# Attention block of one core: P@V for two key tiles in every second step, and products regrouped by odd and even steps

## The reference

```
xn  = layernorm(x)
qkv = xn @ qkv_w + qkv_b                    # 16 heads of 16 channels
a   = softmax(q k^T * 16**-0.5)             # 512 x 512 for each head and row
y1  = (a v) @ proj_w + proj_b
g, u = xn @ w_gate.T / 127, xn @ w_up.T / 127   # integer weights, 768 hidden
y2  = (silu(g) * u) @ w_down.T / 127
out = x + y1 + y2
```

## Time and profile before

| | |
|---|---|
| time before, median of 3 runs | 574.96 us (574.86 to 575.86) |
| the profiled execution | 576.71 us, its span 574.9 us |
| TensorE busy | 97% of the span |
| VectorE, ScalarE, GpSimd busy | 81%, 73%, 53% |
| granted TensorE clock | 0.994 |

### The profile page before, as it was taken

One profiled execution on the slowest core, in us unless ns is written; L12 is line 12 of the kernel. 1 busy time (PEld: TensorE's weight loads), 2 busy tenths in 40 slices (PEclk: granted clock), 3 DMA queues, 4 the chain that ended last, 5 costly groups with the idle time before them and its releaser, 6 DMA issues.

```text
span 574.9 us, 13815 instructions
## 1 busy us (share of the span) xinstructions
PE 555.6 (97%) x4844; PEld 334.2 (58%) x4844; DVE 464.9 (81%) x601; ACT 418.0 (73%) x573; POOL 305.1 (53%) x286
## 2 busy tenths in 40 slices
PE   7898899999999999999999999999999999998896
PEld 6656456565655557556665656555665556554453
DVE  5797777888878888888878889888978888788732
ACT  3666865888668975888668875788758886787572
POOL 3283536755564745755566554846467555355120
PEclk9899989999999999999999999999999999999999
DMA  8896086363854368371872449371873438520101
GB/s 235 254 244 146 3 216 179 57 141 118 236 110 105 62 198 206 56 164 71 245 143 69 98 156 241 62 156 29 228 189 61 93 138 227 99 57 21 57 2 38
DMA packets 55119, 74.89 MB, mean 130 GB/s; under 512 B 5680, under 2 KB 28208, under 8 KB 55088
## 3 DMA queue, kind: packets, MB, share of 16 engines
q1 hardware_dynamic: 55088, 74.47, 52.0%
HBM read 40.90 MB, written 33.03 MB: 129 GB/s over the span
## 4 chain that ended last, share of the span: by engine, by line
PE 90%; DVE 4%; ACT 3%; issue 1%; DMA 1%; SPq 0%; ACTq 0%
PE dense L1280 23%; PE o_bank L1254 22%; PE st_bank L1221 16%; PE dense L1324 14%; PE s_bank L1238 11%; PE dense L1264 2%; DVE neg_max L1004 1%; ACT probs L841 1%; PE dense L1393 1%; DMA probs<-in_L_attn_qkv_w 1%; PE dense L1380 0%; DVE w_dl L1033 0%; PE s_bank L1221 0%; ACT w_qkvh L830 0%; ACT probs L927 0%
## 5 line engine op out<-in xcount | busy, mean ns | idle before, releaser
L1004 DVE TENSOR_REDUCE neg_max<-s_bank 128x2 f32<-128x1024 f32 x250 | 304.9, 1220 | 73.9 <-PE s_bank L1238 72.8
L841 ACT ACTIVATE probs<-st_bank 128x1024 f32<-128x1024 f32 x250 | 256.4, 1026 | 112.6 <-PE st_bank L1221 109.4
L1254 PE MATMUL o_bank<-probs,v_ones 128*32 128x512 f32 x1024 | 137.1, 607 | 0.1
L1221 PEld LDWEIGHTS st_bank<-q_stack,k_stack 50*128 50x128 f32 x500 | 47.7, 184 | 131.7 <-ACT probs L841 82.1
L1221 PE MATMUL st_bank<-q_stack,k_stack 50*128 50x512 f32 x500 | 118.0, 466 | 5.3 <-ACT probs L841 5.0
L1238 PE MATMUL s_bank<-k_stack,q_stack 48*128 48x512 f32 x500 | 108.9, 429 | 0.9 <-DVE neg_max L1004 0.7
L742 POOL TENSOR_TENSOR hid_tl<-gated,hid_th 128x512 fp32r<-128x512 f32 x48 | 61.7, 1285 | 35.2 <-ACT hid_th L941 35.2
L736 POOL TENSOR_TENSOR gated<-gated,hid 128x512 f32<-128x512 f32 x48 | 61.7, 1285 | 28.7 <-DVE gated L1026 19.8
L1280 PE MATMUL dense<-xn_tl,w_gh 64*128 64x512 f32 x176 | 61.9, 391 | 0.0
L1280 PE MATMUL dense<-xn_tl,w_uh 64*128 64x512 f32 x176 | 61.9, 391 | 0.0
L1238 PEld LDWEIGHTS s_bank<-k_stack,q_stack 48*128 48x128 f32 x500 | 47.4, 185 | 20.7 <-DVE neg_max L1004 8.4
(11 more groups left out here) (152 smaller groups left out, 886.2 us busy)
## 6 DMA issues: line engine op xcount, KB each, us to landing
q_stack<-q_spread SPq DMA_DIRECT2D x64, 192.0 KB, 4.7
k_stack<-k_spread SPq DMA_DIRECT2D x64, 192.0 KB, 5.2
q_spread<-qk_parts SPq DMA_DIRECT2D x16, 512.0 KB, 3.8
k_spread<-qk_parts SPq DMA_DIRECT2D x16, 512.0 KB, 3.5
q_spread<-qk_parts SPq DMA_DIRECT2D x16, 256.0 KB, 4.1
k_spread<-qk_parts SPq DMA_DIRECT2D x16, 256.0 KB, 2.0
resid<-in_L_attn_x SPq DMA_DIRECT2D x16, 256.0 KB, 4.3
out<-resid SPq DMA_DIRECT2D x15, 256.0 KB, 2.2
```

Source lines behind the costliest of these rows:

```text
L841: nc.scalar.activation(probs[:, s % 2, 2 * half:2 * half + 2, :], transposed_bank(row, s, half)[:, :, :], ACT.Exp, scale=SCALE).then_inc(e ...
L1004: nc.vector.tensor_reduce(neg_max[:, g % 2, :, NT * pair + qt], score_bank(row, half)[:, :, :], AX_X, ALU.max, negate=True).then_inc(max_d ...
L1221: done = nc.tensor.matmul(transposed_bank(row, s, half)[:, r, :], k_stack[rows, pair, P * kt:P * (kt + 1)], q_stack[rows, pair, :], start= ...
L1254: done = nc.tensor.matmul(o_bank[32 * j:32 * (j + 1), :], v_ones[:, kt, 8 * (g // 2) + 2 * j + g % 2, :], probs[:, (s - 1) % 2, j, :], sta ...
```

## The change

P@V is no longer made in each step. In an even step s `probs_v` is called twice, for the probabilities of step s-2 and of step s-1; an odd step has none. The probabilities' buffer is longer by half a step (`probs_more`), which holds the first half of steps 2, 6, 10 and 14 of a row; `probs_of` picks the place, and the waits of `exp` on `pv_done` follow it. The space comes from `v_bias_rows` and `v_part`, which now lie in `o_norm` and in the second half of `p_part`, with two more waits in `take` that keep them apart.

A product of an odd step is cut in two: its first half is made in `begin_product` (end of the even step), its second half behind `scores` 0 of the odd step; nothing is left before `scores` 0. A product of up with gate or of down that belongs to an even step is made whole ahead of that step's `scores_t` 0: the first half in `begin_product`, the second right behind it. Products in parts of even steps (4, 6 and 8) stay cut as they were.

```diff
-ENDS = {"up": (0, 1)}
...
+        probs_more = sb("probs_more", [P, 2, TOK])
...
+        v_bias_rows = o_norm[:, 0:TOK // 64, :, :].rearrange("p b a d -> p (b a d)").rearrange("p (k n) -> p k n", k=KC)
...
-        v_part = sb("v_part", [P, TOK])
...
+        v_part = p_part[:, 1, :]
...
+        def probs_of(step, half):
+
+            if half == 0 and step % 4 == 2:
+                return probs_more[:, :, :]
+            return probs[:, step % 2, 2 * half:2 * half + 2, :]
...
-                if half == 0 and STEPS * row.like + s >= 2:
-
+                at = STEPS * row.like + s
+                if s % 2 == 0 and half == 0:
+                    if at >= 4:
+                        act.wait_ge(pv_done, STEPS * row.at + s - 3)
+                elif at >= 2 and (s % 2 == 0 or half == 0):
                     act.wait_ge(pv_done, STEPS * row.at + s - 1)
...
+                        if i == 0 and row.like > 0:
+                            act.wait_ge(projected, KC * row.at)
+                        elif row.like > 1:
+                            act.wait_ge(projected, KC * (row.at - 1))
...
+                    if i == 1 and row.has(0):
+                        act.wait_ge(dve_free, count(row, freed_by_dve, kind="v", index=1))
...
-                cut = len(terms) - TWELFTHS // 6 if kind in ("v", "proj") else len(terms) - 1
-                for at in range(cut) if part == 0 else [cut + part - 1 if kind in ("v", "proj") else cut]:
+                odd = chunk[0] % 2 == 1
+                if odd:
+                    cut = len(terms) // 2
+                    pieces = (range(cut), (), range(cut, len(terms)))[part]
+                else:
+                    cut = len(terms) - TWELFTHS // 6 if kind in ("v", "proj") else len(terms) - 1
+                    pieces = range(cut) if part == 0 else [cut + part - 1 if kind in ("v", "proj") else cut]
+                done = None
+                for at in pieces:
                     h, a, b, k = terms[at]
-                    cols = slice(0, TOK) if part == 0 else slice(TOK // 2 * (part - 1), TOK // 2 * part)
+                    whole_width = odd or part == 0
+                    cols = slice(0, TOK) if whole_width else slice(TOK // 2 * (part - 1), TOK // 2 * part)
...
-                ahead, behind = (0, of_all) if long_product(chunk) else ENDS[chunk[2]]
+                ahead, behind = (0, of_all) if chunk[0] % 2 else (of_all, 0)
...
-                    if 0 < STEPS * row.like + s <= STEPS * ROWS:
+                    if s % 2 == 0 and 0 < STEPS * row.like + s <= STEPS * ROWS:
+                        probs_v(row, s - 1)
                         probs_v(row, s)
```

More of the change, by code:

```diff
@@ L276, in build @@
         v_bias = sb("v_bias", [P, KC])
-        v_bias_rows = sb("v_bias_rows", [P, KC, P])
         p_bias = sb("p_bias", [P, C])
@@ L840, in exp @@
                     act.wait_ge(squares_done, 3)
-                nc.scalar.activation(probs[:, s % 2, 2 * half:2 * half + 2, :], transposed_bank(row, s, half)[:, :, :],
+                nc.scalar.activation(probs_of(s, half), transposed_bank(row, s, half)[:, :, :],
                                      ACT.Exp, scale=SCALE).then_inc(exp_done, 1)
@@ L867, in take @@
                                                         kind="v", index=1 - i))
-                        nc.scalar.activation(halves(v_part[:, :]), bank, ACT.Copy).then_inc(act_free, 1)
+                        if i == 0 and row.like > 0:
+                            act.wait_ge(projected, KC * row.at)
+                        elif row.like > 1:
+                            act.wait_ge(projected, KC * (row.at - 1))
+                        nc.scalar.activation(halves(v_part), bank, ACT.Copy).then_inc(act_free, 1)
                         return
@@ L1059, in add_part @@
                     nc.vector.tensor_tensor(v_ones[:, 2 * i:2 * i + 2, :, 0:HD], part.rearrange(apart, t=2, d=HD),
-                                            v_part[:, :].rearrange(apart, t=2, d=HD), ALU.add).then_inc(dve_free, 1)
+                                            v_part.rearrange(apart, t=2, d=HD), ALU.add).then_inc(dve_free, 1)
                 else:
@@ L1254, in probs_v @@
                     done = nc.tensor.matmul(o_bank[32 * j:32 * (j + 1), :], v_ones[:, kt, 8 * (g // 2) + 2 * j + g % 2, :],
-                                            probs[:, (s - 1) % 2, j, :], start=kt == 0, stop=kt == NT - 1,
+                                            probs_of((s - 1) % STEPS, j // 2)[:, j % 2, :], start=kt == 0, stop=kt == NT - 1,
                                             tile_position=(0, 32 * j))
@@ L1497, in chunks @@
                         sum_squares()
-            def long_product(chunk):
-                return chunk[2] == "down"
             def product_at(row, s):
```

## The result

The changed kernel takes 631.38 us (median of 4 runs, 629.76 to 635.9), the kernel before 574.91 beside it (4 runs): a ratio of 1.0987, 95% interval 1.0935 to 1.1038. The forecast was 622, slower by 47; it came out slower by 56. The profiled execution is the longest of the four: 635.9 us, span 634.1, with a mean granted clock of 0.980; the other three have spans of 627.9 to 630.0 at 0.986 to 0.989.

The account below looks back on a forecast made before the run. TensorE, 97% busy, was taken as bound, with the exponentials' and maxima's loops close under it. Rows 1 to 6 +36, row 0 +5, row 7 +6 give +47: 624 us profiled, 622 as median, range 582 to 640.

Parts of the forecast that it names:

- The double: P@V of two key tiles together in an even step, put at 1.92 us; saves 0.28 us of shape changes.
- the floors: Shortest half steps the loops allow: 1.62 us for exponentials, 1.77 for maxima, 1.82 with an addition between two maxima.
- the rival of the switches: Whole kernel: 64 saved tile-shape changes of 0.28 us outweigh waits in odd steps; 559 us, chance 0.07.
- the double saves nothing: Rival on P@V: the second tile pays the same fill and drain as a shape change; 640 us, chance 0.04.
- The table of pairs: Forecast length of each even and odd step pair in a row; row 72.0 us instead of 66.04, +6.0.
- S: Even step, from `scores_t` 0 to `scores_t` 1: 2.48 to 3.11 us, with nothing waiting.
- C: From an even step's `scores_t` 1 to the odd step's `scores` 1: 3.97 us, 3.85 in step 10, 5.05 in step 8.
- the wait between the halves: In even steps' up and down, the second half's first weight load waits for `half_made`: 0.31 us, between 0 and 0.5.
- the sum: Rows 1 to 6 +36, row 0 +5, row 7 +6: +47 us, 624 in profiled terms, 622 as median.
- Only the exponentials' loop binds: Rival: VectorE's jobs, `half_made` and the bank cost nothing; row 66.8, time 585 us, chance 0.16.
- row 7: Last row, with fewer products, near the 1.62 us floor: even steps' first halves grow to about 2.5; +6 us.
- step 9's bank: The next product waits for VectorE's addition to free a shared bank, which ends at 5.05 us instead of running beside P@V.

Follow-up runs that it names:

- e1: Changed kernel with P@V still doubled in even steps, but all products cut and placed as in the kernel before: 632.48 us, 1.0972 of the kernel before.
- e2: Changed kernel with P@V of one key tile in every step, products cut and placed as in the changed kernel: 607.44 us, 1.0559 of the kernel before.
- e8: Changed kernel with exponentials over 256 of 512 queries and maxima over 256 of 512 keys: 587.18 us, 1.0226 of the kernel before.
- e6: Changed kernel with 24 transposes nobody reads, in half steps of row 7 without products: 627.66 us, 1.0934 of the kernel before.
- e3: Changed kernel with the second half of an even step's up or down behind its first transposed scores: 623.95 us, 1.0857 of the kernel before.

## Why the prediction was right, and where its sizes were off

**The mechanism held.** The double saves less than the odd steps lose at the floors. e1 shows it by itself, e2 that the new places are not what rescues it; the rival of the switches (559) is out, and so is "the double saves nothing": it takes 1.86 where two single ones take 2.00, and saves one entry and one follower (0.09 + 0.11) besides, 0.34 a pair where 0.28 stood.

**The table of pairs** came out within 0.33 in every pair. Measured in row 4, from step 0 on: 9.01, 8.13, 8.49, 8.37, 10.90, 9.12, 8.92, 9.45, against 8.92, 8.12, 8.28, 8.55, 11.13, 9.00, 8.92, 9.12. S at step 0 is 2.42 instead of 2.48, the double 1.86 instead of 1.92; C is 3.89 to 4.05 instead of 3.97 (342.74 to 346.79 above; 3.89 in step 10, where 3.85 stood, and 4.91 to the next product in step 8, where 5.05 + 0.10 stood); the wait between the halves costs 0.24 + 0.12 = 0.36 instead of 0.31 in the rows shown. A row takes +6.35 where +6.0 stood, rows 1 to 6 +38.0 for +36, row 0 +5.4 for +5. The half steps of the kernel before, which the prediction put at 1.6 to 2.8, run from 1.62 to 3.20 in row 4; nothing in the sum hangs on it.

**Which loop binds.** "Only the exponentials' loop binds" (585) fell: halving the exponentials gives 0.3 a row, halving the maxima 1.75. With the maxima halved, C is 3.58 to 3.65 in five of the pairs, as that rival had it, but the row 70.63 and not its 66.8: the wait between the halves and step 9's bank, which it put at nothing, stay, two pairs keep an exponential that comes late (C is 3.88 there), and gaps for banks open. The Trainium skill, "TensorEngine Tiling (Array Packing)", section "PSUM Bottleneck", says that tiling makes TensorE faster but not the emptying of PSUM; the runs agree that this emptying binds here: halving what the two readers of the score banks do takes 44.2 us off the changed kernel (631.38 to 587.18; 13.5 of it in row 7, where the granted clock rose too) and 21.8 off the one before (574.91 to 553.15).

**A cost put at nothing.** ScalarE's copy of the odd product was argued free because ScalarE is idle for 0.5 between two exponentials. That is the wrong test. The copy isn't late for ScalarE, it is late for the bank; it costs next to nothing in the changed kernel only because `scores` waits about as long for the maximum, and 2.7 us a row where it doesn't (e8).

**The step that failed in size is row 7**: +6 in the sum, +13.6 measured. Its waits were about right: e6's row, with 24 transposes more and nearly full clock (0.97), is 6.8 over before's. The other 6.7 are the clock, of which the prediction said nothing; the three other executions, with spans 4.1 to 6.2 shorter at a higher clock, probably lose less there, which no trace of them shows. One such stretch of the changed kernel, TensorE at step 4 of row 7, and a second stretch by window:

```profile
573.98 0.50 PE L1255 MATMUL s_bank<-k_stack,q_stack 48*128 48x512 f32 x2 [0.32 <-DVE neg_max L1021]
574.41 0.79 PE L1271 MATMUL o_bank<-probs_more,v_ones 128*32 128x512 f32 x2
...
575.02 2.78 PE L1271 MATMUL o_bank<-probs,v_ones 128*32 128x512 f32 x10
577.72 0.68 PE L1238 MATMUL st_bank<-q_stack,k_stack 50*128 50x512 f32 x2
```

```profile
592.00:598.00 6.00, 5.48 (x24) 1.56 (x24) 2.67 (x3) 1.42 (x2) 0.98 (x2) 0.50 0.27 90
```

The double of step 4 takes 3.31 (574.41 to 577.72) instead of 1.86: 1.45 lost in one place, more than any wait of the loop. With 6.7 more in row 7 and 2 in rows 1 to 6, the sum in the profiled execution's terms would be 633 instead of 624; it took 635.9; the start's 2.1 and small terms are the rest.

## What to carry to other kernels

Where several engines run close to each other, count the shortest time of each half step for every one of them before work is moved together: a saving on the busiest engine is kept only in the half steps that stand above the other engines' floors, and here it was taken out of the ones that were already at it. A resource that looks free because its engine is idle must be asked when its buffer is needed next, not whether its engine has time. And a stretch that gets longer pauses on TensorE should be priced at both clock levels.

## What the runs showed of the hardware that was not expected

The granted clock fell to half inside row 7, in a stretch where TensorE still counts as busy for 56.92 of 65.35 us. Ahead of the first fall (about 574.7) lies a stretch with 15.60 of 17.30 busy at full clock; e2, whose P@V comes every step instead of every second, keeps 1.00 through the whole row with 47.86 of 52.67. So the busy share that the profile shows does not tell the two apart, and neither does the longest pause of TensorE in the row, 0.88 here and 0.97 in e2. Why e6's transposes kept the clock up in the stretch behind them too (589 to 607) was not settled. The four runs' spread follows the clock: spans of 627.9 to 630.0 at 0.986 to 0.989, 634.1 at 0.980.

A matmul whose weight load waits for the matmul just ahead on the same engine starts 0.47 behind it instead of 0.23, and its follower 0.35 behind instead of 0.23. The waits view calls this 0.45 us idle; taking the wait away (e3) gave 0.20 to 0.27.
